# A mixture-of-experts stage in which seven of eight weight chunks are split in two parts instead of six, with one copy moved from VectorE to ScalarE

## The chip, the cores and the metric

The kernel runs as one program on one core of one Trainium2 chip. The metric is the device time of one execution in microseconds; lower is better. Three timed runs of the kernel before gave 2101.71, 2101.75 and 2110.54 us, so its median is 2101.75 us.

## The reference

The program computes four residual blocks over 625 rows of 512 numbers: a hyperbolic graph convolution, a mixture of eight experts, an ordinary graph convolution, and an attention block with a large projection. The change lies in the second block:

```python
x = x + _L0_gnn_ref(_layernorm(x), edge_index, ...)
x = x + _L0_ffn_ref(_layernorm(x)[None], ...)[0]     # the stage of the change
x = x + _L1_gnn_ref(_layernorm(x), edge_index, ...)
x = x + _L1_ffn_ref(_layernorm(x)[None], ...)[0]
# _L0_ffn_ref: 8 experts, each takes the cap = 93 rows with the highest gate weight
probs = softmax(xf @ gate_w.T + gate_b)
sel_w, sel_idx = top_k(wm.T, cap)
xg = xf[sel_idx]
h = gelu(einsum('ecd,edh->ech', xg, w1) + b1, approximate=False)   # 512 -> 2048
out = einsum('ech,ehd->ecd', h, w2) + b2                            # 2048 -> 512
of = zeros.at[sel_idx].add(out * sel_w)
```

## The kernel before

**Chunks.** The weights of an expert are 8 chunks of 1 MB (128 partitions x 2048 float32): four of w1 ("up" chunks 0 to 3) and four of w2 ("down" chunks 0 to 3, which are chunks 4 to 7 of the expert). Over all experts they are counted m = 8 e + c, 0 to 63. SP loads them into eight RAW buffers; the load of chunk m + 8 waits for the semaphore w_used of chunk m, which TensorE raises at the end of chunk m.

**Split and unsplit chunks.** A split chunk has a high part (HW, float32 rounded to the fast fp32r format, made by ScalarE from RAW) and a rest, the low part (LW = RAW - HW, made by VectorE). With the left operand split in the same way, TensorE makes a product of three terms, high x high, low x high and high x low: 12 fp32r matmuls a chunk (moe_parts). An unsplit chunk goes to TensorE as plain float32 straight from RAW and GT. split(m) says which is which: before, down chunks 2 and 3 (m % 8 of 6 and 7) are unsplit. nth and chunk count split chunks in both directions. HW is a ring of four buffers, so the high part of split chunk i waits until split chunk i - 4 is used; LW has eight buffers.

**One expert on TensorE (pe_moe).** up 0, up 1, gelu 0, up 2, gelu 1, up 3, gelu 2, down 0, gelu 3, down 1, dispatch of the next expert (selection matmuls that gather its 93 rows into PSUM bank 6, from PO, XFH, XFL, and the row weights from WSP), down 2, gathered_T of the next expert (four transposes of the gathered rows OT), down 3. "gelu c" on TensorE is four transposes of HS, the result of up c. After up 3 of expert 7 the rows of expert 6 are combined.

**ScalarE (a_moe), in the order of its queue.** For an expert e: up copies PSUM to HS; weights makes a high part HW (two instructions of 1024 columns); gelu makes four Gelu instructions of 94 columns into GT (two buffers, c % 2); dispatch copies the gathered rows to OT, gathered_T makes XGH, the high part of their transpose; scale multiplies the expert's result by the row weights (OW, from expert 6 on OS) after VectorE has added b2.

**VectorE (v_moe), in the order of its queue.** weights makes LW; gelu makes the high part GEH of GT by a copy and the low part GEL by a subtraction; rank_tiles and rank_end rank the tokens for expert e + 2 (five tiles JU and the selection matrix PO), for e up to 5; places() is some bookkeeping in expert 5; dispatch and gathered_T (XGL = low part of the gathered rows); scale adds b2 (OT). In expert 7 it also adds the combined rows (combine(6)), runs degrees and back_low (rows YL gathered back from HBM), v_counts (gCL, the low part of the count matrix for the next stage) and back_high (rows YH).

**GpSimd and SP.** GpSimd issues five indirect gathers into YL after the outputs of experts 0 to 5 are written to HBM (SP's outputs, which wait for scale), and five into YH after chunk 60 has landed.

All of these queues are written out by hand, each engine runs its own strictly in order, and waits are counted semaphores. The overlap of memory that matters for the end: gCH (made by ScalarE, a_counts) and gCL lie over HW0 to HW3, so a_counts and v_counts wait until the last split chunks in those buffers are used.

Of the kernel before, what the change touches and what calls it, by code (L numbers as in the profile page):

```python
# [130 lines left out]
def program(nc, I, out):  # L131
    T5, P, D, NP = 5, 125, 512, 628
    HALF = NP // 2
    MAXN, EPS = 1.0 - 0.004, 1e-15
    NE, CAP, CS = 8, 93, 94
# [5 lines left out]
    with ctx:  # L141
# [11 lines left out]
        def at(name, shape, dt, off):  # L153
            size = 4 if dt in (f32, f32r, i32) else 2
            n = size
            for k in shape[1:]:
                n *= k
            place[name] = off + (n + 31) // 32 * 32
            assert BASE + off + n <= nc.sbuf_usable_end, (name, off, n)
            return nc.alloc_sbuf_tensor_at(name, shape, dt, offset=BASE + off)  # L160

        def after(name):
            return place[name]
# [1034 lines left out]
        XGL = at("XGL", [128, 2, 4 * CS], f32r, after("XGH"))  # L1198
        HS = at("HS", [CS, 2, D], f32, after("XGL"))
        GT = at("GT", [128, 2, 4 * CS], f32, after("HS"))  # L1200
        GEH = at("GEH", [128, 8, CS], f32r, after("GT"))
        GEL = at("GEL", [128, 8, CS], f32r, after("GEH"))
        MU = at("mU", [P, T5, D], f32, after("GT"))
        OT = at("OT", [CS, D], f32, after("mU"))
        B2 = at("B2", [CS, 2, D], f32, after("OT"))
# [52 lines left out]
        turn = (3, 0, 1, 2, 4)  # L1258

        def split(m):  # L1260
            return m % 8 < 6

        def nth(m):
            return 6 * (m // 8) + m % 8

        def chunk(i):
            return 8 * (i // 6) + i % 6

        def moe_parts(m, kk):
            c = slice(512 * kk, 512 * kk + 512)  # L1270
# [70 lines left out]
        def a_moe(q):  # L1341
            def weights(i, halves_=range(2)):
                m = chunk(i)
                if m >= 8 * NE:
                    return
                raw = moe_raw(m)
                q.wait_ge(*landed(N_MOE + m))
                if i < 4:
                    q.wait_ge(*mx_done.of(1, 4))
                    q.wait_ge(*tl_done.of(1, 4))  # L1350
                else:
                    q.wait_ge(*w_used.of(chunk(i - 4)))
                for h in halves_:
                    c = slice(1024 * h, 1024 * h + 1024)
                    q.act(HW[i % 4][:, c], raw[:, c], ACT.Copy).then_inc(*w_hi.up(m, h))
# [55 lines left out]
            def gelu(e, c):  # L1411
                b = 6 + c % 2
                q.wait_ge(*hs_t.of(e, c))
                if c >= 2:
                    q.wait_ge(*gelu_v.of(e, c - 2, "lo"))
                elif e:
                    q.wait_ge(*w_used.of(8 * e - 2 + c))
                else:
                    q.wait_ge(*xfl_done.of(4))
                for j in range(4):  # L1420
                    jj = 16 * e + 4 * c + j
                    g = q.act(GT[:, c % 2, CS * j:CS * j + CS], PS[:, b, CS * j:CS * j + CS], ACT.Gelu, bias=b1T[:, jj:jj + 1])
                g.then_inc(*gelu_a.up(e, c))

            def scale(e):
                k = e % 2
# [12 lines left out]
            gathered_T(0)  # L1439
            rank_row(1)  # L1440
            for e in range(NE):
                n = 6 * e
                up(e, 0)
                weights(n + 4)
                up(e, 1)
                gelu(e, 0)
                weights(n + 5)
                up(e, 2)
                gelu(e, 1)
                weights(n + 6)  # L1450
                up(e, 3)
                if e == NE - 1:
                    a_counts(q)
                gelu(e, 2)
                weights(n + 7)
                gelu(e, 3)
                weights(n + 8)
                if e + 1 < NE:
                    dispatch(e + 1)
                    gathered_T(e + 1)  # L1460
                weights(n + 9)
                scale(e)

        def v_moe(q):
# [90 lines left out]
            def rank_tiles(e, ts_):  # L1555
                k = e % 2
                if e < 2:
                    q.wait_ge(*row_done.of(e))
                    q.wait_ge(*rank_v.of(e, "tail"))
                else:  # L1560
                    q.wait_ge(s_wb[k], 32 * (e // 2))
                for t in ts_:
                    n, w = P * t, WM[:, t, e:e + 1]
                    if 5 * e + t:
                        q.wait_ge(*rank_v.of(*divmod(5 * e + t - 1, 5), "eq"))
                    q.stt(JU[:, 0:625], WB[k][:, :], w, TIEM[:, 500 - n:1125 - n], ALU.subtract, ALU.is_gt, acc=RKA[:, e, t:t + 1]).then_inc(*rank_v.up(e, t, "eq"))
# [29 lines left out]
            def gelu(e, c):  # L1596
                gt = GT[:, c % 2, :].rearrange("p (a b) -> p a b", a=4)
                hi, lo = GEH[:, 4 * c:4 * c + 4, :], GEL[:, 4 * c:4 * c + 4, :]
                q.wait_ge(*gelu_a.of(e, c))
                if e:  # L1600
                    q.wait_ge(*w_used.of(8 * e - 4 + c))
                q.cp(hi, gt).then_inc(*gelu_v.up(e, c, "hi"))
                q.wait_ge(*gelu_v.of(e, c, "hi"))
                q.tt(lo, gt, hi.bitcast(f32), ALU.subtract).then_inc(*gelu_v.up(e, c, "lo"))

            def scale(e):
# [79 lines left out]
            weights(3)  # L1686
            rank_tiles(1, range(3))
            for e in range(NE):
                n = 6 * e
                weights(n + 4)  # L1690
                gelu(e, 0)
                if e == 0:
                    rank_tiles(1, (3, 4))
                    rank_end(1)
                weights(n + 5)
                if e == NB - 1:
                    places()
                if 0 < e < NE - 2:
                    rank_tiles(e + 2, (0, 1))
                gelu(e, 1)  # L1700
                if e == 0:
                    rank_tiles(2, (0, 1))
                weights(n + 6)
                if e + 2 < NE:
                    rank_tiles(e + 2, (2, 3))
                weights(n + 7)
                if e + 2 < NE:
                    rank_tiles(e + 2, (4,))
                    rank_end(e + 2)
                weights(n + 8)  # L1710
                if e + 1 < NE:
                    dispatch(e + 1)
                    gathered_T(e + 1)
                weights(n + 9)
                if e == NE - 1:
                    combine(NE - 2)
                    degrees()
                    back_low()
                    v_counts(q)
                    back_high()  # L1720
                scale(e)

        def pe_moe(q):
# [225 lines left out]
                g_power(q, ln2["rs"][:, t:t + 1], ln2["rs"][:, t:t + 1], hm[0:P, 0:1], ln_pow, 2, t)  # L1949

        def a_counts(q):
            q.wait_ge(*w_used.of(chunk(6 * NE - 3)))
            for m in range(T5):
                q.act(GCH[:, m, :], CT[:, m, :], ACT.Copy).then_inc(*gch_done.up(m))

        def v_counts(q):
            for m in range(T5):
                q.wait_ge(*w_used.of(chunk(6 * NE - (2 if m < 4 else 1))))
                q.wait_ge(*gch_done.of(m))
                q.tt(GCL[:, m, :], CT[:, m, :], GCH[:, m, :].bitcast(f32), ALU.subtract).then_inc(*gcl_done.up(m))  # L1960

# [1259 lines left out]
```

## Time and profile before

| | |
|---|---|
| median of three timed runs | 2101.75 us |
| time of the profiled execution | 2101.96 us |
| its span, first to last instruction | 2100.2 us |
| outside the span | 1.76 us |
| TensorE busy (modelled ends) | 2071.3 us, 99% |
| VectorE busy | 1481.8 us, 71% |
| ScalarE busy | 1127.5 us, 54% |
| mean granted TensorE clock | 0.997 |

The stage of the experts runs from 184.15 us (first matmul of up 0 of expert 0) to 407.6 us (end of down 3 of expert 7), about a tenth of the span. Engine shares of the whole span say little about it; the rows below are all of this stage. A row of a timeline gives start and duration in us, engine, line, instruction, operands and count, and in square brackets the idle time of the engine before it with what ended it. Successive instructions of one engine overlap a little in these rows, so what an instruction takes from a full queue is the distance from its start to the next start, some 0.1 us less than its duration.

### The profile page before, as it was taken

The numbers are of one execution on the slowest core, as the hardware profiler recorded it, in microseconds if no ns is written. First come the engines' busy times: TensorE is split into PE (matmuls) and PEld (weight loads), VectorE is DVE, ScalarE is ACT, GpSimd is POOL, SyncE is SP. The second block draws the span as 40 slices with busy tenths as digits, with TensorE's granted clock in tenths as the row PEclk, the third lists the DMA queues.
The fourth block names the chain that finished last, engine by engine and source line by source line (L and its number), as shares of the span: only waits on it lengthen the run. The fifth ranks groups of instructions, "written<-read, shape, count | busy, mean of one in ns | idle before, by whom it ended". The sixth has DMA issues, their size and how long they took to land.

```text
span 2100.2 us, 35949 instructions
## 1 busy us (share of the span) xinstructions
PE 2071.3 (99%) x13318; PEld 1939.3 (92%) x13318; DVE 1481.8 (71%) x3062; ACT 1127.5 (54%) x3017; POOL 876.5 (42%) x706
## 2 busy tenths in 40 slices
PE   8998999999999999999999999999999999999998
PEld 7976666698899999999999999999999999999997
DVE  8769877754677766767777777666767676766676
ACT  4566676524655554555555555445555555554464
POOL 0010001202555554455555555545555555554461
PEclk9999999999999999999999999999999999999999
DMA  5204998910222211111112221111111122211110
GB/s 141 96 14 142 343 326 298 315 50 9 91 85 90 77 65 65 65 65 65 65 65 77 95 86 65 65 65 65 65 65 65 66 97 88 73 65 65 61 46 25
DMA packets 89161, 201.15 MB, mean 96 GB/s; under 512 B 8196, under 2 KB 12580, under 8 KB 88985
## 3 DMA queue, kind: packets, MB, share of 16 engines
q1 hardware_dynamic: 86746, 196.28, 27.4%
q0 software_dynamic: 2240, 2.57, 0.5%
q8 instruction: 106, 1.74, 0.3%
q14 instruction: 69, 0.57, 0.1%
HBM read 196.31 MB, written 2.51 MB: 95 GB/s over the span
## 4 chain that ended last, share of the span: by engine, by line
PE 95%; DVE 2%; ACT 1%; DMA 0%; POOL 0%; issue 0%; SPq 0%; DVEq 0%; POOLq 0%
PE PS L54 86%; PE PS L53 6%; PE PS L57 4%; DMA X<-in_x 0%; DVE SM L107 0%; POOL SM L60 0%; DVE OHsx L68 0%; ACT mU L88 0%; DVE ACC L60 0%; DVE OHdx L69 0%; DVE X L75 0%; ACT XFH L88 0%; DVE SM L68 0%; DVE U L69 0%; DVE W1L L60 0%
## 5 line engine op out<-in xcount | busy, mean ns | idle before, releaser
L54 PE MATMUL PS<-ZH,WS 128*128 128x314 f32 x4096 | 946.4, 311 | 0.0
L54 PEld LDWEIGHTS PS<-ZH,WS 128*128 128x128 f32 x4096 | 692.3, 189 | 0.0
L54 PE MATMUL PS<-ZL,WS 128*128 128x314 f32 x2048 | 626.2, 306 | 0.0
L60 DVE TENSOR_TENSOR ACC<-ACC,PS 128x314 f32<-128x314 f32 x1008 | 476.3, 477 | 196.8 <-PE PS L54 186.8
L54 PEld LDWEIGHTS PS<-ZL,WS 128*128 128x128 f32 x2048 | 387.6, 189 | 0.0
L60 POOL TENSOR_TENSOR WS<-RAW,WS 128x512 fp32r<-128x512 f32 x256 | 326.9, 1298 | 117.0 <-ACT WS L88 117.0
L60 POOL TENSOR_TENSOR ZS<-ZS,ZQ 128x628 f32<-128x628 f32 x128 | 198.4, 1550 | 231.4 <-ACT ZQ L88 231.3
L60 POOL TENSOR_TENSOR ML<-MF,MH 128x400 fp32r<-128x400 f32 x124 | 130.3, 1051 | 346.8 <-ACT MH L88 346.8
L88 ACT ACTIVATE ZH<-PS,g1T 128x628 fp32r<-128x628 f32 x128 | 100.6, 786 | 314.8 <-PE PS L54 314.8
L88 ACT ACTIVATE EE<-EE,SM 125x100 f32<-125x100 f32 x640 | 233.1, 376 | 1.2 <-DVE SM L68 1.2
L88 ACT ACTIVATE MF<-PS 128x400 f32<-128x400 f32 x128 | 64.7, 506 | 303.7 <-PE PS L53 303.7
L75 DVE SCALAR_TENSOR_TENSOR ZL<-PS,g1T,ZH 128x628 fp32r<-128x628 f32 x128 | 111.6, 872 | 118.5 <-ACT ZQ L88 118.5
L60 POOL TENSOR_TENSOR WQ<-RAW,WQ 128x512 fp32r<-128x512 f32 x128 | 168.0, 1312 | 43.4 <-ACT WQ L88 43.4
L60 DVE TENSOR_TENSOR EE<-PS,CB 125x400 f32<-125x400 f32 x160 | 91.9, 575 | 126.7 <-PE PS L54 125.8
L60 DVE TENSOR_TENSOR EE<-EE,SM 125x500 f32<-125x500 f32 x128 | 154.9, 1210 | 4.4
L88 ACT ACTIVATE WS<-RAW 128x512 fp32r<-128x512 f32 x256 | 147.6, 633 | 0.0
L88 ACT ACTIVATE ATH<-PS 100x500 fp32r<-100x500 f32 (+1 forms) x256 | 96.6, 430 | 94.2 <-PE PS L57 94.2
L54 PE MATMUL PS<-MH,XH 128*125 128x400 f32 x640 | 143.7, 346 | 0.0
L54 PE MATMUL PS<-MH,XL 128*125 128x400 f32 x640 | 142.7, 344 | 0.0
L54 PE MATMUL PS<-ML,XH 128*125 128x400 f32 x640 | 142.3, 344 | 0.0
L60 DVE TENSOR_TENSOR LW<-RAW,HW 128x1024 fp32r<-128x1024 f32 x96 | 113.2, 1220 | 32.5 <-ACT HW L88 32.4
L53 PEld LDWEIGHTS PS<-KCL,WQ 128*128 128x128 f32 x1024 | 129.7, 191 | 2.4 <-issue 1.5
(361 smaller groups left out, 3545.9 us busy)
## 6 DMA issues: line engine op xcount, KB each, us to landing
RAW<-in_L_ffn_wz_w SPq DMA_DIRECT2D x66, 1024.0 KB, 5.7
RAW<-in_L_ffn_w SPq DMA_DIRECT2D x64, 1024.0 KB, 6.2
RAW<-in_L_ffn_Wq_w SPq DMA_DIRECT2D x32, 1024.0 KB, 8.3
CB<-c_rows SPq DMA_DIRECT2D x32, 195.3 KB
RAW<-in_L_gnn_W SPq DMA_DIRECT2D x4, 1024.0 KB, 16.5
RAW<-in_L_ffn_Wkv_w SPq DMA_DIRECT2D x4, 1024.0 KB, 14.8
RAW<-in_L_ffn_Wk_T SPq DMA_DIRECT2D x2, 1024.0 KB, 17.5
WB<-w_rows SPq DMA_DIRECT2D x6, 273.4 KB
```

The lines of the kernel that those rows point to most:

```text
L53: return self.q.matmul(o, l, r, start=start, stop=stop, skip_group_check=True)
L54: return self.q.matmul(o, l, r, start=start, stop=stop)
L57: return Nothing() if self.q is None else self.q.transpose(o, i, idn)
L60: return Nothing() if self.q is None else self.q.tensor_tensor(out=o, in0=a, in1=b, op=op)
L75: return self.q.scalar_tensor_tensor(out=o, in0=a, scalar=s, in1=b, op0=op0, op1=op1)
L88: return self.q.activation(o, i, f, **kw)
```

## The change

1. split(m) is m % 8 < 7: down chunk 2 of each expert is split too; only down chunk 3 stays plain float32. GEH and GEL grow from 8 to 12 blocks, nth and chunk count seven a group, and each engine's list has one more weights call (n + 10) an expert.
2. The copy GEH of a Gelu chunk is made by ScalarE, right behind the four Gelu instructions, for c = 0, 1, 2; VectorE only subtracts, for c = 0, 1 and now also 2.
3. On ScalarE the next expert's dispatch (OT) and gathered_T (XGH) stand behind two weights calls after gelu 3 instead of one; on VectorE the gathered rows' rest XGL stands ahead of the last two weights calls, where it stood ahead of the last one.
4. In expert 7, VectorE's combine(6) moves ahead of its new gelu 2, a_counts moves behind gelu 3 on ScalarE, and VectorE makes four of the five gCL tiles before back_high and the fifth after it. Their waits name down 0, down 1 and down 2 of expert 7 where they named up 3, down 0 and down 1.

```diff
-        GEH = at("GEH", [128, 8, CS], f32r, after("GT"))
-        GEL = at("GEL", [128, 8, CS], f32r, after("GEH"))
+        GEH = at("GEH", [128, 12, CS], f32r, after("GT"))
+        GEL = at("GEL", [128, 12, CS], f32r, after("GEH"))
...
         def split(m):
-            return m % 8 < 6
+            return m % 8 < 7
...
         # a_moe
                 if c >= 2:
                     q.wait_ge(*gelu_v.of(e, c - 2, "lo"))
+                elif e and c == 0:
+                    q.wait_ge(*gelu_v.of(e - 1, 2, "lo"))
                 elif e:
-                    q.wait_ge(*w_used.of(8 * e - 2 + c))
+                    q.wait_ge(*w_used.of(8 * e - 1))
...
                 g.then_inc(*gelu_a.up(e, c))
+                if split(8 * e + 4 + c):
+                    if e:
+                        q.wait_ge(*w_used.of(8 * e - 4 + c))
+                    q.wait_ge(*gelu_a.of(e, c))
+                    q.act(GEH[:, 4 * c:4 * c + 4, :], GT[...], ACT.Copy).then_inc(*gelu_a.up(e, c, "hi"))
...
                 up(e, 3)
-                if e == NE - 1:
-                    a_counts(q)
                 gelu(e, 2)
                 weights(n + 7)
                 gelu(e, 3)
+                if e == NE - 1:
+                    a_counts(q)
                 weights(n + 8)
+                weights(n + 9)
                 if e + 1 < NE:
                     dispatch(e + 1)
                     gathered_T(e + 1)
-                weights(n + 9)
+                weights(n + 10)
                 scale(e)
...
         # v_moe
             def gelu(e, c):
-                q.wait_ge(*gelu_a.of(e, c))
+                q.wait_ge(*gelu_a.of(e, c, "hi"))
...
-                q.cp(hi, gt).then_inc(*gelu_v.up(e, c, "hi"))
-                q.wait_ge(*gelu_v.of(e, c, "hi"))
                 q.tt(lo, gt, hi.bitcast(f32), ALU.subtract).then_inc(*gelu_v.up(e, c, "lo"))
...
                 weights(n + 6)
                 if e + 2 < NE:
                     rank_tiles(e + 2, (2, 3))
+                if e == NE - 1:
+                    combine(NE - 2)
+                gelu(e, 2)
                 weights(n + 7)
...
                 weights(n + 9)
+                weights(n + 10)
                 if e == NE - 1:
-                    combine(NE - 2)
                     degrees()
                     back_low()
-                    v_counts(q)
+                    v_counts(q, range(4))
                     back_high()
+                    v_counts(q, (4,))
                 scale(e)
```

## Rows read from the trace of the kernel before

**Rows 1.** The page: busy time and share of TensorE.

```profile
PE 2071.3 (99%) x13318; PEld 1939.3 (92%) x13318; DVE 1481.8 (71%) x3062; ACT 1127.5 (54%) x3017; POOL 876.5 (42%) x706
```

**Rows 2.** The chain that ended last, experts 3 and 4: start, us, what.

```profile
273.53 0.33 PE PS L57 x4
273.85 2.78 PE PS L54 x12
...
301.38 0.32 PE PS L57 x4
```

**Rows 3.** TensorE's timeline, down 2 and what follows it, expert 3.

```profile
288.48 3.60 PE L54 MATMUL PS<-RAW,GT 128*94 128x512 f32 x8
291.92 0.49 PE L57 MATMUL PS<-ident,OT 94*128 94x94 f32 x4
```

**Rows 4.** ScalarE's timeline, expert 3.

```profile
271.28 2.00 ACT L88 ACTIVATE HW<-RAW 128x1024 fp32r<-128x1024 f32 x2
...
274.06 1.00 ACT L88 ACTIVATE GT<-PS,b1T 128x94 f32<-128x94 f32 x4
274.95 2.01 ACT L88 ACTIVATE HW<-RAW 128x1024 fp32r<-128x1024 f32 x2
276.85 0.60 ACT L88 ACTIVATE HS<-PS 94x512 f32<-94x512 f32 x1
...
288.68 0.59 ACT L88 ACTIVATE OT<-PS 94x512 f32<-94x512 f32 x1 [2.35 <-PE PS L54]
292.44 0.48 ACT L88 ACTIVATE XGH<-PS 128x376 fp32r<-128x376 f32 x1 [3.17 <-PE PS L57]
292.82 1.99 ACT L88 ACTIVATE HW<-RAW 128x1024 fp32r<-128x1024 f32 x2
296.89 0.72 ACT L88 ACTIVATE OW<-OT,SM 94x512 f32<-94x512 f32 x1 [2.08 <-DVE OT L60]
```

**Rows 5.** VectorE's timeline, expert 3.

```profile
272.36 2.36 DVE L60 TENSOR_TENSOR LW<-RAW,HW 128x1024 fp32r<-128x1024 f32 x2 [3.35 <-ACT HW L88]
...
275.49 0.55 DVE L60 TENSOR_TENSOR GEL<-GT,GEH 128x376 fp32r<-128x376 f32 x1
276.05 2.36 DVE L60 TENSOR_TENSOR LW<-RAW,HW 128x1024 fp32r<-128x1024 f32 x2
278.32 0.87 DVE L76 SCALAR_TENSOR_TENSOR JU<-WB,WM,TIEM 125x625 f16<-125x625 f32 x1
...
280.03 0.35 DVE L91 CAST GEH<-GT 128x376 fp32r<-128x376 f32 x1
...
288.04 0.99 DVE L68 TENSOR_SCALAR PO<-io,RKA 125x94 fp32r<-125x94 f32 x5
...
296.18 0.68 DVE L60 TENSOR_TENSOR OT<-PS,B 94x512 f32<-94x512 f32 x1
```

**Rows 6.** ScalarE's timeline, the two high parts of expert 6 that waited for a load.

```profile
373.23 2.00 ACT L88 ACTIVATE HW<-RAW 128x1024 fp32r<-128x1024 f32 x2 [4.67 <-DMA RAW<-in_L_ffn_w]
...
379.89 2.01 ACT L88 ACTIVATE HW<-RAW 128x1024 fp32r<-128x1024 f32 x2 [2.33 <-DMA RAW<-in_L_ffn_w]
```

**Rows 7.** Windows: length, busy (count) PE, PEld, DVE, ACT, POOL, clock, DMA share, GB/s.

```profile
356.00:360.00 4.00, 4.00 (x22) 2.84 (x21) 3.13 (x4) 3.73 (x9) 0.89 (x1) 1.00 1.04 394
...
364.00:368.00 4.00, 4.00 (x22) 2.85 (x21) 3.06 (x4) 4.00 (x11) 2.68 (x2) 1.00 1.04 253
```

**Rows 8.** VectorE's timeline, the end of expert 7.

```profile
392.71 3.08 DVE L60 TENSOR_TENSOR X<-X,PS 125x512 f32<-125x512 f32 x5
...
404.33 3.10 DVE L60 TENSOR_TENSOR X<-X,YH 125x512 f32<-125x512 f32 x5 [1.42 <-DMA YH<-y_rows,IH]
407.65 0.69 DVE L60 TENSOR_TENSOR OT<-PS,B 94x512 f32<-94x512 f32 x1 [0.22 <-PE PS L54]
```

**Rows 9.** TensorE's timeline before expert 0: filler matmuls after an idle stretch.

```profile
173.51 4.58 PE L54 MATMUL PS<-HW 128*94 128x512 f32 x12 [2.95 <-DVE JU L76]
```

**Rows 10.** The window in which they began, columns as in the windows above.

```profile
174.00:176.00 2.00, 2.00 (x7) 1.30 (x6) 1.93 (x5) 0.00 (x0) 0.00 (x0) 0.61 0.09 18
```

More of the change, by code:

```diff
@@ L1260, in split @@
         def split(m):
-            return m % 8 < 6
+            return m % 8 < 7
         def nth(m):
-            return 6 * (m // 8) + m % 8
+            return 7 * (m // 8) + m % 8
         def chunk(i):
-            return 8 * (i // 6) + i % 6
+            return 8 * (i // 7) + i % 7
         def moe_parts(m, kk):
@@ L1423, in gelu @@
                 g.then_inc(*gelu_a.up(e, c))
+                if split(8 * e + 4 + c):
+                    if e:
+                        q.wait_ge(*w_used.of(8 * e - 4 + c))
+                    q.wait_ge(*gelu_a.of(e, c))
+                    q.act(GEH[:, 4 * c:4 * c + 4, :], GT[:, c % 2, :].rearrange("p (a b) -> p a b", a=4), ACT.Copy).then_inc(*gelu_a.up(e, c, "hi"))
             def scale(e):
@@ L1441, in a_moe @@
             for e in range(NE):
-                n = 6 * e
+                n = 7 * e
                 up(e, 0)
@@ L1688, in v_moe @@
             for e in range(NE):
-                n = 6 * e
+                n = 7 * e
                 weights(n + 4)
@@ L1951, in a_counts, with v_counts @@
         def a_counts(q):
-            q.wait_ge(*w_used.of(chunk(6 * NE - 3)))
+            q.wait_ge(*w_used.of(chunk(7 * NE - 3)))
             for m in range(T5):
                 q.act(GCH[:, m, :], CT[:, m, :], ACT.Copy).then_inc(*gch_done.up(m))
-        def v_counts(q):
-            for m in range(T5):
-                q.wait_ge(*w_used.of(chunk(6 * NE - (2 if m < 4 else 1))))
+        def v_counts(q, ms):
+            for m in ms:
+                q.wait_ge(*w_used.of(chunk(7 * NE - (2 if m < 4 else 1))))
                 q.wait_ge(*gch_done.of(m))
```

## The prediction

> **What bounds the kernel now.** I read the page first, then the chain of work that ended last inside the experts' stage, then TensorE's, ScalarE's and VectorE's timelines of one expert, the waits of the stage, and windows of the DMA load. The page says TensorE is busy 99% of the span [rows 1]. The chain says more: through the stage it is TensorE's own queue without a break, and expert 3 takes from one set of transposes at 273.53 to the same set at 301.38, 27.85 us [rows 2]. So a matmul less is time less, as long as ScalarE and VectorE still deliver. Their timelines show slack of two kinds: ScalarE waits 2.35 us for TensorE before OT and 3.17 us before XGH [rows 4], VectorE waits 3.35 us for ScalarE before the LW of down 0 [rows 5]. In expert 6 ScalarE waits 4.67 and 2.33 us for the loads of chunks 58 and 59 [rows 6]. At the end of expert 7 VectorE comes free 0.22 us before down 3 ends [rows 8]: it has no slack there at all, and the last OT is what TensorE's combine(7) waits for.
>
> **TensorE's gain.** An unsplit down 2 takes 291.92 - 288.48 = 3.44 us for its eight matmuls [rows 3], a split chunk 2.78 us for twelve, 0.23 us each [rows 2]. Gain 0.66 us an expert, 5.3 us over eight; the period would be 27.19 us. The Trainium skill, page "TensorE: Matmul & The Clock Gate", section "Back-to-back issue gap", gives about 131 ns as the sustained spacing of matmuls of 512 columns in a stream with weight loads. By it a split chunk would take 1.6 us and the change would bring 15 us, to about 2087. This case's trace does not agree: 0.23 us each in chunks of the very kind that is added, and that decides.
>
> **What is added elsewhere.** ScalarE gets one more HW, 1.90 us from start to next start, and three GEH copies. It has none now; the nearest row is XGH, of the same shape, 0.48 us long and 0.38 to the next start [rows 4]. A GEH must wait for the end of the last Gelu, 1.00 after the first start where the next HW now starts at 0.89, so it costs 0.11 + 0.04 + 0.38 = 0.53. Bounds: 0.38, if nothing has to drain, and 0.7, if a copy behind its own engine's semaphore gets no overlap; I take 0.53. That is 1.90 + 1.6 = 3.5 us more an expert. VectorE gets one more LW, 276.05 to 278.32 = 2.27, one more GEL, 0.55 long, 0.46 to the next start, and loses two casts of 0.35 [rows 5]: about 2.0 more.
>
> **ScalarE and VectorE form a loop.** VectorE's OT releases ScalarE's scale, HS of up 0 stands behind that, and VectorE's first LW behind the HW after it. I count from the start of that HS, called h, after the change. ScalarE: HS 0.49 (0.60 less the overlap), HW to 2.39, HS, Gelu from 2.88, GEH at 3.92, HW of down 1 at 4.30; an LW can start 1.08 after its HW (271.28, 272.36 [rows 4, 5]), so LW of down 1 starts at 5.4. From there VectorE has no gap left: six LW of 2.27 are 13.6; five rank tiles and PO are 2 x 1.71 (278.32 to 280.03) + 0.91 + 0.90 = 5.2; two GEL 0.9; the weights' two small instructions and XGL 0.8 (an estimate from GEL's length); OT 0.68. That ends at h + 26.6, and the next h is 0.72 - 0.06 = 0.66 later [rows 4, 5]: 27.3 us. TensorE wants 27.2. The loop that had more than a microsecond of slack becomes the bound by 0.1 us an expert, and any lateness it collects stays.
>
> How late may h be? Continuing ScalarE's list, HS of up 3 starts at h + 10.0 and ends at 10.6, the next OT copy runs from h + 18.5 to 19.1. TensorE wants the first at 14.8 after its own up 0 began (four ups of 2.78, three transpose sets of 0.33, down 0), the second at 23.4. So h may be 4.1 to 4.2 us behind the start of up 0, and 2.8 is the least, as HS waits for up 0.
>
> - **Expert 0** ranks two tiles and a PO more (2.6 us). Reckoned through in the same way, h of expert 1 is 5.4 us behind up 0: TensorE stalls 1.3 us, on the transposes of gelu 0 and gelu 3.
> - **Experts 2 to 4** lose 0.1 us each, **expert 5** 0.5, because places() puts about 1.5 us (my estimate for eleven small instructions one behind the other) ahead of gelu 1 on VectorE.
> - So up 0 of expert 6 begins 6 x 0.66 - 1.3 - 0.3 - 0.5, about 2 us earlier than before.
>
> **Expert 6.** On ScalarE OT now stands behind the HW of chunk 58, which has no data before 373.23 [rows 6]. The loads are slow there: 394 GB/s in 356 to 360 us, 253 in 364 to 368 with the gathers into YL in flight, at a DMA share of 1.04 in both [rows 7]. The gathers wait for the outputs of expert 5, which wait for ScalarE's scale, so for the loop, which is no earlier than before (up 0 is 2 us earlier, h of expert 6 at 4.7 instead of 2.8 us behind it); SP sits in front of those outputs, so the loads behind them start no earlier either. I take the landings of chunks 58 and 59 as unchanged. Bounds: they move with TensorE, 2 us earlier, or come 1 us later. Then OT ends about 376.4 as before, TensorE stalls 2 us in front of gathered_T(7), and the 2 us are gone. LW of chunk 59 starts 379.89 + 1.08, OT follows 2.27 later, 0.68 long, and h of expert 7 is 384.6, as before. The Trainium skill, page "DMA: Bandwidth & Descriptors", section "SWDGE vs HWDGE vs iDMA", says that each DMA engine takes turns between its queues; the trace agrees, in that GB/s fall while the DMA share stays at 1.04.
>
> **Expert 7.** VectorE after h: LW of down 1 ends at 7.7, GEL 1 waits for its GEH (8.25), LW of down 2 for its HW (9.2) and ends at 11.5. From combine(6) to OT it took 407.65 - 392.71 less idle 1.42 and 0.22 = 13.3 [rows 8]; with GEL 2, 13.7. OT starts at h + 25.2 = 409.8 where it started at 407.65: 2.1 us late. The wait for YH (404.33 [rows 8]) lies before back_high's new turn at 406 and costs nothing now. Down 3 ends near 407, so TensorE stands, but for 2 us of key matmuls, until combine(7), and everything behind shifts. a_counts waits for down 0 of expert 7 and is off the path: gCH is done by h + 18, VectorE wants it at 18.5.
>
> **Sum.** 2101.96 - 4.0 (six experts) + 2.1 (their stalls) + 1.9 (expert 6's loads) + 2.1 (VectorE at the end) = **2104.0 us**, against 2101.96 of the profiled execution, which is 0.2 above the median.
>
> **Rivals.**
> 1. The loads of chunks 58 and 59 move with TensorE: h of expert 7 is 2 us earlier, the last OT starts at 407.6, **2101.9**. For it: in expert 6 they are issued on TensorE's semaphores. Against: rows 7 and SP's order. 0.23.
> 2. Nothing outside TensorE binds, the whole 5.3 us come through: **2096.6**. For it: the average shares, 71% and 54%. Against: VectorE's last stretch would need 4 us of slack it doesn't show [rows 8]. 0.12.
> 3. The clock: TensorE stands for over 3 us ahead of combine(7). Before expert 0 it stood 2.95 us, the granted clock was 0.61 of full in the next window (the lower of its two levels for most of it) and twelve fillers took 4.58 us [rows 9, 10] where twelve at 0.23 take 2.8: 1.8 more. **2106**, or 2108 if it falls in expert 6's stall too. 0.12.
> 4. Slower: the overlap of instructions does not hold on the fuller queues. If each takes its full duration, 0.1 us more, and GEH 0.7, the loop is about 29 us, 1.2 above the old period: +6 over five experts, 1.3 after expert 0, and about 4 in the last stretch of VectorE, **2113**. It decides from a loop of 27.9 on. Against: HW, LW and Gelu keep that overlap in their densest stretches now [rows 4, 5]. 0.05.
> 5. The added matmuls come closer together than 0.23 us. At 0.18 the gain is 3.44 - 2.16 = 1.28 us an expert and 10.2 in all, **2092**. Against: 0.23 in every split chunk of the chain. 0.01. The Trainium skill's figure quoted above is this rival at its strongest.
>
> **How the numbers follow.** The forecast has 0.47, the likeliest. The range 2097 to 2109 holds it, rivals 1 and 3 and the bounds (GEH 0.1 off is 0.5 over five experts, landings 1 us later is +1), and the edge of rival 2. About 0.5%, 10.5 us, is what a measurement of this kernel can tell from no change. Faster by more needs twice TensorE's whole gain, rival 5 or something unnamed: 0.02. Slower by more is rival 4 beyond 2112.5: 0.05. Within: 0.93.
>
> **What the profile after would show.** Down 2 as twelve matmuls in 2.78 us; GEH as ScalarE instructions of 0.48 us; VectorE's wait before the LW of down 0 about as long, that before XGL gone; experts 2 to 4 at 27.2 to 27.3 us a period; ScalarE's OT 0.3 us after it is wanted or later in expert 1 and 2 us in expert 6; TensorE idle about 3 us before combine(7), released by OSL. If HW of chunk 58 starts before 372, or VectorE's OT of expert 7 waits for TensorE, the sum is wrong on the high side; if a period is above 27.9, on the low side.

## The result and the profile after

The changed kernel takes 2108.8 us, the median of 20 runs (2104.99 to 2118.83), against 2100.65 us of the kernel before on the same chip (20 runs, 2098.03 to 2110.54). The ratio is 1.0042, 95% interval 1.0034 to 1.005: a small loss, 8 us of the medians, where 2104.0 had been forecast, 2 us above the profiled execution of before. The profiled execution of the changed kernel took 2105.53 us.

The page of the changed kernel, its head line and the busy times, shows nearly the same shares as before [rows 1], 32 TensorE instructions more and 4.3 us less of TensorE's work:

```profile
span 2103.8 us, 36082 instructions
PE 2067.0 (98%) x13350; PEld 1942.1 (92%) x13350; DVE 1497.6 (71%) x3070; ACT 1153.0 (55%) x3057; POOL 879.4 (42%) x706
```

So the added matmuls did save TensorE time, and the time went into waits. TensorE's timeline of expert 2 shows the one that comes back in most experts (a row: start, duration, engine, line, operands, count, in brackets the idle time before it and what ended it):

```profile
244.57 0.49 PE L57 MATMUL PS<-ident,HS 94*128 94x94 f32 x4
...
257.65 0.55 PE L54 MATMUL PS<-WSP,PO 125*94 125x2 f32 x5 [0.47 <-ACT GT L88]
...
260.42 0.39 PE L54 MATMUL PS<-HW,GEH 128*94 128x512 f32 x1
...
263.20 0.49 PE L57 MATMUL PS<-ident,OT 94*128 94x94 f32 x4
```

Down 2 takes 263.20 - 260.42 = 2.78 us for its twelve matmuls, as forecast from [rows 2]; before it was 3.44 [rows 3]. But the first matmuls of dispatch (into WSP's PSUM bank 7, which gelu 3's transposes used last) wait for ScalarE's last Gelu. The kernel before has no such wait. Here it is 0.25 us in expert 0 (at 200.22), 1.06 in expert 1 (229.68), 0.47 to 0.53 in experts 2 to 4, none in expert 5 and 0.42 in expert 6. What follows from it is seen on ScalarE, experts 3 and 4:

```profile
270.59 0.57 ACT L88 ACTIVATE HS<-PS 94x512 f32<-94x512 f32 x1
...
274.48 0.52 ACT L88 ACTIVATE GEH<-GT 128x376 fp32r<-128x376 f32 x1
274.90 1.99 ACT L88 ACTIVATE HW<-RAW 128x1024 fp32r<-128x1024 f32 x2
...
284.46 1.00 ACT L88 ACTIVATE GT<-PS,b1T 128x94 f32<-128x94 f32 x4
...
291.69 0.48 ACT L88 ACTIVATE XGH<-PS 128x376 fp32r<-128x376 f32 x1 [1.96 <-PE PS L57]
...
297.92 0.73 ACT L88 ACTIVATE OW<-OT,SM 94x512 f32<-94x512 f32 x1 [3.86 <-DVE OT L60]
298.55 0.58 ACT L88 ACTIVATE HS<-PS 94x512 f32<-94x512 f32 x1
```

and on VectorE:

```profile
292.20 0.55 DVE L60 TENSOR_TENSOR XGL<-PS,XGH 128x376 fp32r<-128x376 f32 x1 [0.65 <-ACT XGH L88]
292.67 4.62 DVE L60 TENSOR_TENSOR LW<-RAW,HW 128x1024 fp32r<-128x1024 f32 x4
297.21 0.68 DVE L60 TENSOR_TENSOR OT<-PS,B 94x512 f32<-94x512 f32 x1
```

Read them as one ring, that is a chain of waits that comes back to where it began, so that its length is the period of an expert: HS at 270.59 (the h of the forecast), last Gelu done and WSP at 285.61 (h + 15.0), XGH at h + 21.1, XGL, two more low parts, OT at h + 26.6, the scale OW, and the next h at 298.55: 27.96 us. VectorE stands 0.65 us ahead of XGL, inside the stretch that the forecast had taken as gapless.

In expert 6 ScalarE waits for chunks 58 and 59 as before [rows 6], and OT, now behind the first of them, holds TensorE:

```profile
374.12 2.01 ACT L88 ACTIVATE HW<-RAW 128x1024 fp32r<-128x1024 f32 x2 [2.14 <-DMA RAW<-in_L_ffn_w]
376.03 0.72 ACT L88 ACTIVATE PT<-PS 94x500 fp32r<-94x500 f32 x2
376.65 0.59 ACT L88 ACTIVATE OT<-PS 94x512 f32<-94x512 f32 x1
...
380.74 2.01 ACT L88 ACTIVATE HW<-RAW 128x1024 fp32r<-128x1024 f32 x2 [2.38 <-DMA RAW<-in_L_ffn_w]
```

TensorE's three waits at the end of the stage:

```profile
377.29 0.54 PE L57 MATMUL PS<-ident,OT 94*128 94x94 f32 x4 [1.42 <-ACT OT L88]
...
397.78 0.51 PE L57 MATMUL PS<-ident,HS 94*128 94x94 f32 x4 [2.47 <-DVE X L60]
...
413.22 0.47 PE L54 MATMUL PS<-OS,PT 94*125 94x512 f32 x1 [1.06 <-DVE OSL L75]
```

The middle one had not been foreseen: gelu 2 of expert 7 needs the PSUM bank that combine(6) on VectorE empties, and that addition now stands behind the low part of down 2. VectorE to the last OT, beside [rows 8]:

```profile
394.67 2.36 DVE L60 TENSOR_TENSOR LW<-RAW,HW 128x1024 fp32r<-128x1024 f32 x2 [0.40 <-ACT HW L88]
396.95 3.07 DVE L60 TENSOR_TENSOR X<-X,PS 125x512 f32<-125x512 f32 x5
...
404.22 2.98 DVE L60 TENSOR_TENSOR gCL<-CT,gCH 125x628 fp32r<-125x628 f32 x4 [0.21 <-PE PS L54]
407.12 3.09 DVE L60 TENSOR_TENSOR X<-X,YH 125x512 f32<-125x512 f32 x5
410.13 0.80 DVE L60 TENSOR_TENSOR gCL<-CT,gCH 125x628 fp32r<-125x628 f32 x1
410.85 0.68 DVE L60 TENSOR_TENSOR OT<-PS,B 94x512 f32<-94x512 f32 x1
```

**Where the time went.** I compare the times at which TensorE transposes gelu 0 of each expert, from its timeline in both profiles, and its first matmul of combine(7):

| from, to | before | after | difference | forecast |
|---|---|---|---|---|
| gelu 0 of expert 0 to that of expert 6 | 167.75 | 168.99 | +1.2 | -2.0 |
| gelu 0 of expert 6 to that of expert 7 | 28.39 | 30.31 | +1.9 | +2.0 |
| gelu 0 of expert 7 to combine(7) | 24.16 | 26.57 | +2.4 | +2.1 |

The sum is 5.5 us (5.6 for the stage from its first matmul: 225.87 to 231.47). Behind the first matmul of combine(7) nothing has changed: from there to the end of the time it is 1691.9 us before and 1692.3 after. The profiled execution of the changed kernel entered the stage 2.4 us earlier than that of before, which is chance: the stretch of low clock ahead of the stage lies elsewhere in it, and a second profile of the same kernel (below) lacks most of that. The medians are 8.15 us apart, 2.6 more than the stage explains; experiment 5 bears on that.

### The profile page after: what moved, and what is told of

Same layout as the page of the kernel before. It is cut to its first block, busy times and chain, and to the rows that moved or that the text cites. A ratio compares the mean times of both kernels' runs of the same rounds, so it can differ in the third digit from the quotient of the medians.

```text
span 2103.8 us, 36082 instructions
## 1 busy us (share of the span) xinstructions
PE 2067.0 (98%) x13350; PEld 1942.1 (92%) x13350; DVE 1497.6 (71%) x3070; ACT 1153.0 (55%) x3057; POOL 879.4 (42%) x706
## 4 chain that ended last, share of the span: by engine, by line
PE 88%; DVE 5%; ACT 4%; DMA 1%; issue 1%; POOL 0%; SPq 0%; DVEq 0%; ACTq 0%; POOLq 0%
PE PS L54 78%; PE PS L53 6%; PE PS L57 4%; ACT HW L88 2%; DVE LW L60 1%; ACT GT L88 1%; DMA RAW<-in_L_ffn_w 1%; DVE JU L76 0%; DMA X<-in_x 0%; ACT HS L88 0%; DVE SM L107 0%; POOL SM L60 0%; ACT GEH L88 0%; DVE X L60 0%; DVE OHsx L68 0%
## 5 line engine op out<-in xcount | busy, mean ns | idle before, releaser
L60 DVE TENSOR_TENSOR LW<-RAW,HW 128x1024 fp32r<-128x1024 f32 x112 | 131.4, 1219 | 20.2 <-ACT HW L88 20.2
```

The costliest lines, as they stand in the source:

```text
L60: return Nothing() if self.q is None else self.q.tensor_tensor(out=o, in0=a, in1=b, op=op)
```

## The experiments

Experiments 1 to 8 are the changed kernel with at most one edit, 9 to 12 join several; each is compared with the kernel before on the same chip. The code shown is cut to the lines that matter; the conditions in the lists of the engines that follow from them are left out. "Stage" is TensorE's time from the first matmul of up 0 of expert 0 to that of combine(7): 225.87 us before, 231.47 after. The period is the time from one expert to the next on TensorE, 27.85 before.

**1. The changed kernel again**, no edit.

> The changed kernel once more, unedited, for a second profile and for the spread of its times. Theory A (the stage): from the first matmul of expert 0 to combine(7) it takes 231.5 us as in the first profile, against 225.9 before; the loop of ScalarE and VectorE has a period of 27.96 us. Theory B (the clock): the stage is as long in each run, but the runs that are slower than 2105.5 us have a lower granted clock somewhere, and this profile shows a second stretch at the low level; 0.001 less in the mean clock goes with about 2 us. If A alone held, all runs would lie near 2105.5 us and not at a median of 2108.8.

Measured: 2108.14 us (2104.9 to 2111.67, 5 runs), ratio 1.004 (1.0026 to 1.0053). The profile of a 2107.77 us run has a stage of 231.96 and began it at 183.52, against 184.15 before. So the stage's 5.5 to 6 us stand, and the earlier start of the first profile was chance.

**2. gelu3_early**, the ring over dispatch opened:

```diff
                 gelu(e, 2)
-                weights(n + 7)
                 gelu(e, 3)
+                weights(n + 7)
```

> On ScalarE gelu 3 ahead of weights(n + 7) instead of behind it; nothing else. Theory A says that dispatch on TensorE waits for the last Gelu, which frees PSUM bank 7, and that this makes the period of experts 1 to 4 27.96 instead of 27.3 us. Then the wait of TensorE before the WSP matmuls (0.5 to 1.1 us an expert) and that of VectorE before XGL (0.65 us) go, and the period is 27.2 to 27.4 us; about 2.5 to 3 us less by expert 5. At the end only what the loads of chunks 58 and 59 do not take back: 0 to 3 us less than the changed kernel. Rival (the loop is VectorE's sum of work alone): period unchanged near 27.96, time unchanged.

Measured: 2105.39 us (2104.0 to 2107.85, 8 runs), ratio 1.0024 (1.0014 to 1.0035). TensorE has no wait ahead of WSP, and the period is 270.99 - 243.74 = 27.25 us:

```profile
243.74 0.49 PE L57 MATMUL PS<-ident,HS 94*128 94x94 f32 x4
...
256.18 0.50 PE L54 MATMUL PS<-WSP,PO 125*94 125x2 f32 x5
...
261.69 0.49 PE L57 MATMUL PS<-ident,OT 94*128 94x94 f32 x4
...
270.99 0.49 PE L57 MATMUL PS<-ident,HS 94*128 94x94 f32 x4
```

That is the 27.2 to 27.3 us of the forecast, so the wait on the last Gelu is what made 27.96 of it. TensorE's own 27.2 and the loop's 27.3 are too close to say which of them sets it now, but the loop closes at this length. From gelu 0 of expert 0 to that of expert 6 it takes 165.89 us, 3.1 less than the changed kernel and 1.9 less than before, where the forecast had 2.0 less. These 3 us are not kept: chunk 58 lands 190.4 us behind the start of the stage, 1.9 earlier, TensorE stands 3.17 us ahead of gathered_T(7), and the granted clock falls to its lower level (windows of the same kernel: length, busy (count) of PE, PEld, DVE, ACT, POOL, clock, DMA share, GB/s):

```profile
375.80 0.54 PE L57 MATMUL PS<-ident,OT 94*128 94x94 f32 x4 [3.17 <-ACT OT L88]
376.18 5.29 PE L54 MATMUL PS<-RAW,GT 128*94 128x512 f32 x8
```

```profile
376.00:380.00 4.00, 4.00 (x9) 1.48 (x8) 2.92 (x4) 1.68 (x3) 0.00 (x0) 0.57 1.05 344
```

Down 3 takes 5.29 us there, 3.60 at the full clock. The stage is 231.80, no shorter, though the median is 3 us lower.

**3. geh_vector**, the copy GEH back on VectorE:

```diff
             # a_moe, gelu: no copy; v_moe, gelu:
+                q.cp(hi, gt).then_inc(*gelu_v.up(e, c, "hi"))
+                q.wait_ge(*gelu_v.of(e, c, "hi"))
                 q.tt(lo, gt, hi.bitcast(f32), ALU.subtract)...
```

> The copy GEH goes back to VectorE, all else as in the changed kernel. Then ScalarE's GT of gelu 3 ends 1.6 us earlier (three copies of 0.5), so TensorE's dispatch waits less, but VectorE has 3 x 0.39 more and the two copies whose wait now falls away. My working: from h, LW of down 1 can start at 4.85 instead of 5.4, then 21.2 + 1.2 of work: h to h 27.9 us, about as now. So periods of experts 2 to 4 between 27.6 and 28.1 and the time within 2 us of the changed kernel; at the end VectorE has 0.4 us of GEH more and the last OT is 0.3 to 0.8 us later. Rival: moving the copy is what costs (0.53 us each on ScalarE, 24 of them); then this kernel is 4 us or more faster than the changed one.

Measured: 2104.71 us (2102.75 to 2109.8, 7 runs), ratio 1.0022 (1.0011 to 1.0033). The first three periods are 28.56, 27.58 and 27.45, and there is no wait at WSP. The working had 27.9; taking the copies away from ScalarE brings the last Gelu forward, and in the period that is worth more than the casts cost VectorE. The median is 4 us below the changed kernel's, as the rival said. But this profile doesn't show those 4 us in the stage, which is 231.98: 1.7 us are gained up to expert 6 and 2.0 in expert 7, and 4.2 are lost in expert 6, where TensorE stands 3.62 us for chunk 58 and the clock is 0.50 behind it.

**4. scale_later**, ScalarE's scale behind the high part of down 0, so that HS of up 0 does not wait for VectorE:

```diff
                 up(e, 0)
                 weights(n + 4)
+                if e:
+                    scale(e - 1)
...
-                scale(e)
+                if e == NE - 1:
+                    scale(e)
```

> ScalarE's scale of expert e - 1 is moved behind HS of up 0 and the HW of down 0 of expert e, so that ScalarE no longer waits for VectorE's OT before them. Theory A: the loop is cut there; ScalarE starts HS 2.8 us after up 0 began instead of up to 5.7, VectorE waits under 1 us for the LW of down 0 instead of 2.2, and the period in experts 1 to 4 is TensorE's own, 27.2 us; stage 3 to 5 us shorter unless the loads of chunks 58 and 59 take it back, the end of expert 7 as in the changed kernel. Rival (VectorE's work alone is too much): its sum is 24.4 us an expert, so it would not bind; the rival predicts 27.9.

Measured: 2109.76 us (2107.52 to 2110.78, 5 runs), ratio 1.0047 (1.0033 to 1.0061). HS of up 0 now waits for TensorE alone (3.83 us at 267.07), yet WSP still waits 0.49 us (at 254.78) and the period is still 27.93 (241.71 to 269.64): the scale's 0.6 us have only moved into ScalarE's list ahead of the last Gelu, and the ring now closes over TensorE. The rival's number, 27.9, came true, but not its reason: VectorE stands idle for 3.8 us a period (four waits of 0.40 to 1.59), so its work doesn't bind. With experiment 2 this says which wait held the period: not VectorE's OT by itself but how late ScalarE's last Gelu is. The stage, forecast 3 to 5 us shorter, is 234.74, 3.3 longer: TensorE stands 3.68 us ahead of gathered_T(7) and the clock is 0.50 behind it.

**5. filled**, useless matmuls in TensorE's two long waits, five ahead of gathered_T(7) and eight ahead of gelu 2 of expert 7:

```diff
+                if e == NE - 2:
+                    for _ in range(5):
+                        q.mm(PS[0:94, 1, :], xf[:, 0:94], xf[:, 0:512], True, True)
                 if e + 1 < NE:
                     gathered_T(e + 1)
...
+                    q.wait_ge(*hs_done.of(e, 2))
+                    for _ in range(8):
+                        q.mm(PS[0:94, 0, :], xf[:, 0:94], xf[:, 0:512], True, True)
                 gelu(e, 2)
```

> The changed kernel with filler matmuls into free PSUM banks in two stalls of TensorE: 5 (1.2 us) before gathered_T of expert 7, where it stands 1.4 to 2.0 us, and 8 (1.8 us) before the transposes of gelu 2 of expert 7, where it stands 2.3 to 2.5 us. They are shorter than the stalls, so they add nothing to the path. Theory B (the clock falls in these stalls in most runs, as it does in the profiles of the three edited kernels): the median goes from 2108 to about 2105.5 us or less and the highest runs lose most. Rival (the slower runs come from the stretch before the experts, where the clock is also low in each profile): median and spread stay as in the changed kernel, 2108 and 2105 to 2112.

Measured: 2106.18 us (2104.62 to 2117.11, 11 runs), ratio 1.0033 (1.0022 to 1.0043). The stage is as long (231.43), but nine of the eleven runs lie between 2104.6 and 2107.4, with a median of 2105.7 and mean granted clocks of 0.997 and 0.998. The changed kernel's 25 runs, the three of 2115.66 and above left out, lie between 2104.9 and 2112.2, with a median of 2108.2, and 16 of these 22 have a mean clock of 0.995 to 0.997. So filling the two waits is worth about 2 us (the kernel before was 0.6 us faster on this chip too), and it goes with a higher clock. That the clock falls behind those two waits in ordinary runs is the likely reading; it isn't shown, for both profiles of the changed kernel, of a run of 2105.53 and one of 2107.77, have the full clock through the whole stage. The other two runs took 2115.75 and 2117.11. One of them is the profiled one, and it shows a granted clock of 0.50 to 0.77 from 516 to 540 us, far behind the stage, in code that no edit touches. More on that in experiments 11 and 12.

**6. last_unsplit**, only chunk 62 (down 2 of expert 7) plain float32 again:

```diff
-            return m % 8 < 7
+            return m % 8 < 7 and m != 62
```

> Chunk 62, down 2 of expert 7, is left unsplit, so VectorE loses one LW and one GEL in the last expert. Theory A: VectorE's last OT starts 2.7 to 3.2 us earlier, within 0.5 us of the end of down 3, and combine(7) with it: the whole kernel 2.5 to 3 us faster than the changed one in the stage. Theory B adds that TensorE's idle stretch of over 2 us before combine(7) shrinks below 1 us; if the low clock comes from there, the median falls by more than 3 us and the spread shrinks. If the path at the end is another (gCH, YH), the gain is under 1 us.

Measured: 2104.5 us (2102.99 to 2106.55, 11 runs), ratio 1.0019 (1.001 to 1.0028), 4 us less than the changed kernel. From gelu 0 of expert 7 to combine(7) it takes 24.15 us, 2.4 less than the changed kernel and as long as before, and the wait for combine(6) is gone too. The profile's stage is still 231.43, for it lost the 2.4 us in expert 6, with a wait of 2.08 us and the clock at 0.72 behind it. VectorE's last OT is at 409.52 and waits for TensorE:

```profile
409.52 0.69 DVE L60 TENSOR_TENSOR OT<-PS,B 94x512 f32<-94x512 f32 x1 [0.15 <-PE PS L54]
```

**7. order_e6**, in expert 6 ScalarE's OT and XGH ahead of the high part of chunk 58:

```diff
+                if e != NE - 2:
+                    weights(n + 9)
                 if e + 1 < NE:
                     dispatch(e + 1)
                     gathered_T(e + 1)
+                if e == NE - 2:
+                    weights(n + 9)
```

> In expert 6 alone, ScalarE's dispatch and gathered_T stand ahead of the HW of chunk 58. Theory A2: the stall before gathered_T(7) is nothing but the OT copy queued behind that HW. It goes, TensorE reaches up 0 of expert 7 about 1.4 to 2 us earlier, but VectorE's LW of chunk 59, and so OT(6) and h of expert 7, still wait for chunk 59, so the last OT stays where it is: TensorE's time goes into a longer stall elsewhere in expert 7, and the stage changes by less than 0.7 us. Rival: TensorE's progress sets the end, and the kernel is 1.5 to 2 us faster.

Measured: 2109.85 us (2108.49 to 2117.05, 4 runs), ratio 1.0043 (1.0027 to 1.0058). The wait ahead of gathered_T(7) is gone and comes back: 1.75 us ahead of gelu 0 of expert 7 (386.76, for HS) and 2.96 ahead of gelu 2, with a clock of 0.63 in 400 to 404 us. So what TensorE lost to the landing of the chunks it loses whichever instruction stands behind it. The stage is 233.87, 2.4 us longer, where it was to change by less than 0.7.

**8. outputs_later**, SP writes an expert's outputs not behind the load that down 3 releases but behind that of the next expert's up 1:

```diff
-                if m % 8 == 7 and m // 8 < NB:
-                    outputs(m // 8)
+                if m % 8 == 1 and 0 < m // 8 <= NB:
+                    outputs(m // 8 - 1)
```

> SP issues the outputs of expert e behind the load that up 1 of expert e + 1 releases, instead of ahead of the load that up 0 releases; so the loads of chunks 56 and 57 do not stand behind ScalarE's scale. Theory C: chunk 58 lands 18 to 19 us after the loads behind those outputs are issued, in all six profiles, so it lands with SP's queue and not with TensorE. Then here it lands 1 to 3 us earlier against up 0 of expert 6, the stall before gathered_T(7) is under 0.7 us instead of 1.4 to 2.0, and chunk 59 comes 1 to 3 us earlier too; stage 1 to 3 us shorter. Rival (the gathers set the landing): the gathers start as late as now, chunk 58 lands within 0.7 us of where it did, nothing is gained.

Measured: 2113.39 us (2105.9 to 2115.07, 4 runs), ratio 1.0053 (1.0034 to 1.0072). In the profile chunk 58 is no longer waited for, nor is OT:

```profile
369.43 3.91 ACT L88 ACTIVATE HW<-RAW 128x1024 fp32r<-128x1024 f32 x4
373.23 0.74 ACT L88 ACTIVATE PT<-PS 94x500 fp32r<-94x500 f32 x2
373.85 0.60 ACT L88 ACTIVATE OT<-PS 94x512 f32<-94x512 f32 x1
```

So the landing of chunk 58 hangs on SP's order, as the forecast said: SP stands in front of outputs(5) with the loads behind it, and the gathers into YL (from 358.63 us in the changed kernel, from 364.29 here) then share the DMA engines with them. Which of the two counts, the loads issued earlier or the gathers later, this run can't tell. The stage is 230.61, only 0.9 us shorter, since TensorE still waits 1.76 us for combine(6). The median is worse: three of the four runs took 2113.27 to 2115.07 at a mean clock of 0.991 to 0.993, and the profiled one of them has a clock of 0.50 from 516 to 532 us, behind the stage.

**9. split_six**, chunks 54 and 62 plain float32, gelu 3 early:

```diff
-            return m % 8 < 7
+            return m % 8 < 7 and m not in (54, 62)
```

> Down 2 of experts 0 to 5 stays split in two parts, down 2 of experts 6 and 7 (chunks 54 and 62) is plain float32 again, and ScalarE's gelu 3 stands ahead of the high part behind it as in gelu3_early. It leaves out the part of the change whose gain the last two experts can't keep. Theory A (the change pays 0.6 us an expert as long as the loop over dispatch is open, and only the end of the stage takes it back): TensorE reaches expert 6 about 3 us earlier than before, waits 2 to 3.5 us ahead of gathered_T(7) because chunk 58 lands where it always does, and VectorE's last OT starts where it did before (407.65) or up to 1 us later: 2101 to 2103. Theory B (something else in the changed program costs time, whatever the last experts do): 2105 or more, as gelu3_early and last_unsplit had it.

Measured: 2101.35 us (2100.09 to 2102.43, 10 runs), ratio 0.9999 (0.999 to 1.0009), the same as before. The stage is 226.22. TensorE waits 1.78 us ahead of gathered_T(7), OT of expert 7 is at 407.09. Where only six experts have the split, nothing is lost at the end, but the loads take back in expert 6 what was gained.

**10. split_six_out**, the same with outputs later.

> As split_six, and SP issues the outputs of an expert behind the load that up 1 of the next expert releases, as in outputs_later. Theory A: chunks 58 and 59 then land 2 to 4 us earlier, TensorE doesn't wait ahead of gathered_T(7), and the 3 us gained in experts 1 to 5 come through to combine(7): stage some 223 us, 2098 to 2099, if the clock stays up in the stretch behind 508 us; where it falls there the run is 9 us longer. Rival: the gathers into YH and YL, which then start later, end up ahead of back_low or back_high: VectorE waits for YL or YH in expert 7 and OT(7) starts at 408 or later, 2101 or more.

Measured: 2099.77 us (2096.83 to 2107.8, 10 runs), ratio 1.0004 (0.999 to 1.0018). TensorE does not wait for gathered_T(7), the stage is 224.04. Seven runs lie at 2096.8 to 2100.4, three at 2106.2 to 2107.8 with a mean granted clock of 0.992 to 0.994.

**11. unsplit62_out**: gelu 3 early, only chunk 62 plain, outputs later.

> Only chunk 62 is plain float32, gelu 3 stands ahead on ScalarE, outputs later: the change with its three found waits eased. Theory A: periods of 27.25 us, no wait for chunk 58, OT of expert 7 waits for TensorE alone, stage 223 to 225 us, 2098 to 2101 in runs without a low clock in or behind the stage. Rival (the wait moves on to the next buffer, as with order_e6): TensorE waits again 1.5 to 3 us in expert 7, stage 228 or more, 2103 or more.

Measured: 2105.81 us (2096.17 to 2107.84, 7 runs), ratio 1.0012 (0.9994 to 1.0029). The stage is 223.84, 2.0 us shorter than before and 7.6 shorter than after: the change does pay there once its waits are eased. Yet four of seven runs are at 2105.8 or above, at a clock of 0.992 to 0.994, three at 2096.17 to 2100.2. The profile, of a run of the upper group, shows where the time goes; TensorE's timeline and the windows:

```profile
505.64 0.86 PE L54 MATMUL PS<-KCF,bqT 128*16 128x100 f32 x8 [0.59 <-ACT KCF L88]
506.91 2.62 PE L53 MATMUL PS<-KCL,WQ 128*128 128x200 f32 x16 [0.41 <-DVE KCL L60]
509.33 1.99 PE L54 MATMUL PS<-XP,RAW 128*128 128x100 f32 x8
```

```profile
504.00:508.00 4.00, 3.00 (x26) 2.53 (x26) 0.60 (x3) 1.04 (x2) 0.00 (x0) 1.00 0.00 0
508.00:512.00 4.00, 4.00 (x19) 3.65 (x18) 1.63 (x3) 1.81 (x4) 0.00 (x0) 0.50 0.08 24
```

Behind two short waits the granted clock is half for some 20 us, and eight matmuls of XP take 1.99 us instead of 1.10.

**12. late_filled**, the same with fillers in those two waits:

```diff
             for g in range(4):
                 keys(g)
+            pe_busy(q, 0, GUH[:, 0, :], 3)
             bias_rows(0)
+            pe_busy(q, 0, GUH[:, 0, :], 2)
```

> As unsplit62_out, whose seven runs fell apart in two groups (2096.17 to 2100.20 and 2105.81 to 2107.84) and whose profile shows the granted clock at 0.50 from 508 to 528 us; added are three filler matmuls where TensorE waits 0.59 us for KCF and two where it waits 0.41 us for KCL, some 4 us ahead of that stretch. They are work without a use and cost at most 0.15 us. Theory A (the clock falls there because TensorE has short idle stretches in that place): the group at 2106 and above is gone, all runs lie at 2096 to 2101, the profile shows 1.00 from 500 to 530 us, and the ratio to before lies below 1. Theory B (the fall comes with the moment at which the stretch is reached, or from something else, and the idle there has no part in it): a third to a half of the runs stay at 2105 to 2108, and the median is 2100 or more.

Measured: 2098.61 us (2097.24 to 2100.27, 12 runs), ratio 0.9983 (0.997 to 0.9996). No run of twelve is in the upper group, and the windows stay at the full clock:

```profile
504.00:508.00 4.00, 4.00 (x28) 3.15 (x28) 0.00 (x0) 1.01 (x2) 0.00 (x0) 1.00 0.00 0
508.00:512.00 4.00, 4.00 (x35) 3.63 (x32) 1.67 (x6) 1.85 (x5) 0.00 (x0) 1.00 0.02 4
```

This version is the only one here that is measurably faster than the kernel before, by 0.17%.

## Why the prediction was wrong

**The failed step: "So h may be 4.1 to 4.2 us behind the start of up 0".** (By the forecast's own four times it is 4.2 and 4.3.) The forecast asked what TensorE needs of ScalarE and found HS of up 3 and OT. It left out dispatch, whose first matmuls need bank 7, which the last Gelu reads. TensorE wants it 18.0 us after its up 0 began (four ups and two downs of 2.78, four transpose sets of 0.33), the last Gelu is done at h + 15.0: the limit is 3.0, not 4.1. The forecast had h at its limit from expert 1 on, so the wait came in those experts; it came in expert 0 as well. It also closed the second ring, over gathered_T, XGH and XGL, in which VectorE gets a gap of 0.65 us: 27.96 instead of 27.3. Shown by gelu3_early (ring opened, 27.25), geh_vector (Gelu earlier, 27.45 and no wait) and scale_later (HS freed from OT, no change). Over experts 0 to 5 the stage missed the forecast by 3.2 us, all but 0.3 of its 3.5, and gelu3_early gets 3.1 of them back. The forecast named the sign itself: a period above 27.9.

**The second term: the clock, put at nothing in the sum.** The forecast missed the median by 4.8 us: 3.5 in the stage and 2.6 by which the ordinary runs lie above what the profiled stage explains, less the 1.3 by which its base of 2101.96 lay above the median of before. The 2.6 go with a lower mean clock, and filling TensorE's two waits takes about 2 of them away (experiment 5). Where in an ordinary run the clock falls was not seen.

**Right:** the twelve matmuls in 2.78 us; GEH, put at 0.53 with its wait, starts 1.04 us after the Gelus and the next HW 0.42 behind it, so it costs 274.90 - 273.44 - 0.89 = 0.57; the loop without the ring, 27.3 and measured 27.25 (TensorE alone would give 27.2); and the 1.9 us more in expert 6. This last number is right for partly other reasons: TensorE's wait ahead of gathered_T(7) is 1.42 us where 2 had been put, and the landings, taken as unchanged, came 0.9 us later, and measured from the start of the stage 3.3 us later (192.37 against 189.08), since the outputs that SP waits for hang on the slower period. They come 17.9 to 19.1 us after the loads issued behind outputs(5) in all profiles with that order.

**The tail:** h to the last OT was put at 25.2 us and took 25.4 (385.45 to 410.85). The OT is 3.2 us late instead of 2.1, because h of expert 7 came 0.85 later. The unforeseen wait of 2.47 us for combine(6) cost nothing on top, for VectorE, not TensorE, ends this stretch; it only shortened TensorE's wait at the end from the 3 us expected to 1.06. VectorE waits 2.22 us before the low part of down 0, not "about as long" as 3.35 [rows 5].

**The rivals.** Rival 1 (loads move with TensorE) and 2 (nothing else binds) are out; outputs_later shows that SP's order decides on the loads. Rival 3 (the clock) was given 0.12. As it was written, with over 3 us of standing ahead of combine(7), it did not happen: the wait is 1.06 us and the clock stays up. Its other half, expert 6's stall, is in four profiles of variants with a low clock behind gathered_T(7)'s wait, and in neither profile of the changed kernel. With the 2 us of experiment 5 its chance was too small and its price about right, as far as the runs show. Rival 4 had the sign and the point from which it decides ("a loop of 27.9 on", and 27.96 was measured), by another mechanism than the loss of overlap it named: an HW still takes 1.90 us to the next start (274.90 to 276.80). The time of 2108.8 lies inside the range of 2097 to 2109 by 0.2 us, which is luck, and within 0.5% of before. The likeliest case missed it by 4.8 us, more than twice the loss of 2.0 us that it forecast, and the loss is one that the runs can tell from nothing.

**What stays open.** A few runs of both kernels (before: five of 95, 2109.35 to 2110.54; after: three of 25, 2115.66 to 2118.83) lie 7 to 10 us above the others. Those whose clock is listed have a mean of 0.990 to 0.993, like the four profiled runs with a low clock somewhere in 508 to 540 us. In those four the time behind combine(7) is 1701.3 to 1701.8 us, in the other ten 1691.9 to 1692.3: the low stretch costs 9.4 us. Experiments 11 and 12 show that the idle there has a part in it, as far as 4 of 7 runs against none of 12 can show it. Why it falls in some executions and not in others with the same rows was not found, nor was such a run of the kernels before and after profiled. That the changed kernel is hit more often isn't shown, and the fillers of experiment 12 were not tried in the kernel before, so how much of its 0.17% is owed to the change is open. Nor is it known why geh_vector's median is 4 us lower with a stage as long.

## What to carry to other kernels

Before a bound such as "this may be so late" is used, list every instruction of the waiting engine that names the late one's results or its buffers, PSUM banks first: here the binding one was a five-matmul group of 0.5 us that waited for a bank, not for data. When a change takes 0.66 us a turn from the bound engine and adds 3.5 to another, look for the ring that closes, and price it by its own sum; the share of busy time (55%) says nothing of it. Where a change leaves new waits on TensorE, look at the granted clock behind them and behind the short waits further on, in more than one run, and try fillers: here 1.0 us of waiting went with 20 us at half the clock, which cost 9.4.

## What the runs showed of the hardware

- **A few short idles can halve the clock for 20 us.** In unsplit62_out TensorE was busy 3.00 of 4 us (0.59 and 0.41 us idle), with full clock for over 100 us ahead, and was then granted 0.50 from 508 to 528 us. It is so in some executions and not in others with the same two waits: split_six_out and the changed kernel have the same 3.00 of 4 and kept 1.00. It cost 9.4 us a run; with five fillers it was in none of 12 runs, without them in 4 of 7. The Trainium skill, page "TensorE: Matmul & The Clock Gate", section "A second HAM failure mode: psum-queue depth-cycling", says that frequent micro-idles between groups of matmuls can make the clock fall and rise. The trace agrees that idles well under 1 us can come ahead of a fall; here it was two of them and a single fall of 20 us.
- **The length of a single wait doesn't decide on the clock.** Ahead of gathered_T(7), in expert 6, the clock of 376 to 380 us was 0.57, 0.50 and 0.50 after waits of 3.17, 3.62 and 3.68 us (down 3 took 5.3 to 6.2 us there instead of 3.60) and 0.72 after 2.08, but 1.00 after 1.42, 1.78 (split_six) and 2.02 (experiment 1). Ahead of gelu 2 of expert 7 it stayed at 1.00 after 2.47 and 2.33 us (both profiles of the changed kernel) and was 0.62, 0.61 and 0.63 in a window soon behind waits of 1.49 (gelu3_early), 1.76 (outputs_later) and 2.96 (order_e6).
- **With GpSimd's gathers in flight the DMA engines move fewer bytes** without being less busy: 269 GB/s in 364 to 368 us of the changed kernel and 381 in 380 to 384, at a DMA share of 1.04 in both, as in [rows 7].
